# Attention pipeline of a two-layer gated cross-attention kernel: from four stages to five, on one Trainium2 core

## The reference

```python
x = x + jnp.tanh(g_xattn[0]) * _L0_xattn_ref(_layernorm(x, axis=-1), ctx_1024, ...)   # rotated q and k
x = x + jnp.tanh(g_ffn[0]) * _L0_ffn_ref(...)      # 8 experts, best 2 of 8
x = x + jnp.tanh(g_xattn[1]) * _L1_xattn_ref(...)  # normed context, gated result
x = x + jnp.tanh(g_ffn[1]) * _L1_ffn_ref(...)      # ternary weights
```

## Time and profile before

| | us |
|---|---|
| median of 3 runs | 3047.76 (3045.49 to 3053.43) |
| the profiled execution, own time | 3043.93 |
| its span, first to last instruction | 3042.1 |
| busy PE, DVE, ACT, POOL in the span | 2019.0, 1762.6, 1315.4, 1003.7 |
| mean granted clock of PE | 0.809 |
| layer 0 attention, first statistics to last result | 12.07 to 786.6 |
| layer 1 attention, likewise | 1552.1 to 2345.1 |

### The profile page before, as it was taken

One profiled execution on the slowest core, in us unless ns is written; L12 is line 12 of the kernel. 1 busy time (PEld: TensorE's weight loads), 2 busy tenths in 40 slices (PEclk: granted clock), 3 DMA queues, 4 the chain that ended last, 5 costly groups with the idle time before them and its releaser, 6 DMA issues. The chain is left out here.

```text
span 3042.1 us, 49795 instructions
## 1 busy us (share of the span) xinstructions
PE 2019.0 (66%) x14617; PEld 1560.7 (51%) x14617; DVE 1762.6 (58%) x3650; ACT 1315.4 (43%) x2345; POOL 1003.7 (33%) x1096
## 2 busy tenths in 40 slices
PE   5777677777543199999938788887886334444443
PEld 4555555555433199999825566665664222222222
DVE  5666666666454233333225555555553898988887
ACT  3444333344211044444324444444443566666665
POOL 0000100001266522222243333333330465565554
PEclk8988888888655599999968999999998566666666
DMA  2111111110443322222243333333331000000000
GB/s 68 40 36 43 36 39 36 37 43 26 141 154 125 123 76 87 87 87 87 77 82 65 69 80 71 69 68 67 76 70 56 17 27 28 28 21 28 28 25 17
DMA packets 177265, 185.56 MB, mean 61 GB/s; under 512 B 23745, under 2 KB 170946, under 8 KB 176130
## 3 DMA queue, kind: packets, MB, share of 16 engines
q1 hardware_dynamic: 152578, 149.49, 16.5%
q0 software_dynamic: 24576, 34.62, 5.6%
HBM read 109.82 MB, written 74.24 MB: 61 GB/s over the span
## 5 line engine op out<-in xcount | busy, mean ns | idle before, releaser
L527 DVE TENSOR_REDUCE a_mneg<-a_ps_s 128x8 f32<-128x960 f32 x256 | 285.8, 1151 | 63.0 <-PE a_ps_s L681 62.5
L681 PE MATMUL a_ps_s<-a_k,a_q 96*128 96x240 bf16 x1024 | 189.5, 334 | 153.9 <-DVE a_of L538 149.6
L377 ACT ACTIVATE a_probs<-a_ps_s 120x1024 f32<-120x1024 f32 x256 | 250.2, 1018 | 84.3 <-PE a_ps_s L695 84.3
L1295 DVE TENSOR_TENSOR e_h<-e_s,e_ps_ab 128x256 f32<-128x256 f32 (+1 forms) x213 | 89.4, 420 | 293.4 <-ACT e_s L1121 293.4
L1086 POOL TENSOR_TENSOR e_h_lo<-e_h 128x256 bf16<-128x256 f32 (+1 forms) x213 | 130.2, 611 | 326.0 <-DVE e_h L1295 326.0
L1314 PE MATMUL e_ps_ab<-e_xt_hi,e_w_hi 128*128 128x256 bf16 (+1 forms) x852 | 232.8, 273 | 0.1
L1314 PE MATMUL e_ps_ab<-e_xt_hi,e_w_lo 128*128 128x256 bf16 (+1 forms) x852 | 232.7, 273 | 0.0
L1314 PE MATMUL e_ps_ab<-e_xt_lo,e_w_hi 128*128 128x256 bf16 (+1 forms) x852 | 232.7, 273 | 0.0
L313 POOL TENSOR_TENSOR a_ve<-a_mv,a_eps 128x2 f32<-128x2 f32 x32 | 6.2, 195 | 664.7 <-DVE a_mv L506 664.7
L681 PEld LDWEIGHTS a_ps_s<-a_k,a_q 96*128 96x128 bf16 x1024 | 118.0, 121 | 195.2 <-DVE a_of L538 104.8
L341 POOL DMA_INDIRECT a_xa<-back_rows,a_where x128 | 202.2, 1580 | 45.8 <-issue 44.3
(11 more groups left out here) (237 smaller groups left out, 5430.8 us busy)
## 6 DMA issues: line engine op xcount, KB each, us to landing
e_xe<-sent_rows SPq DMA_DIRECT2D x71, 272.0 KB, 2.8
back_rows<-e_yo SPq DMA_DIRECT2D x71, 256.0 KB, 2.1
x_rows<-a_x SPq DMA_DIRECT2D x64, 256.0 KB, 3.2
a_xa<-in_x SPq DMA_DIRECT2D x32, 256.0 KB, 2.7
a_xr<-in_x SPq DMA_DIRECT2D x32, 256.0 KB, 2.9
e_xa<-x_rows SPq DMA_DIRECT2D x8, 1024.0 KB, 10.6
a_xa<-x_rows SPq DMA_DIRECT2D x32, 256.0 KB, 2.8
x_rows<-a_xa SPq DMA_DIRECT2D x32, 256.0 KB, 2.6
```

The costliest lines, as they stand in the source:

```text
L377: nc.scalar.activation(probs[0:S, 4 * g:4 * g + 4, :].rearrange("p h n -> p (h n)"), ps_s[0:S, g % 2, :, :].rearrange("p a n -> p (a n)"), ...
L527: nc.vector.tensor_reduce(mneg[:, g // 2, 8 * (g % 2):8 * (g % 2) + 8].rearrange("p (a h) -> p a h", a=2), ps_s[:, g % 2, :, 0:4 * S].rear ...
L681: last = nc.tensor.matmul(ps_s[:, g % 2, j // 2, (j % 2) * 2 * S:(j % 2 + 1) * 2 * S], q2[0:96, back.par, c, t * P:(t + 1) * P], k2[0:96, ...
```

## The change

The stages become *pre*, *front*, *mid*, *back*, *tail* (and *soon* in layer 1). The max scores, their maxima and the turning of the maxima are *mid*, a step ahead of *back*. The normed rows are transposed and copied at the end of *pre*, into `xt`, which now has two buffers; in layer 1 the gate projection is computed in *mid*. `ps_s` is split into `ps_m` for max scores and `ps_e` for scores and products, two banks each; the turned product goes to `ps_t` and `ps_x`. Max scores, maxima, scores and exponentials are done in eight groups of half the size rather than four. POOL takes over `xn` (and `cn`, the normed context of layer 1) and, in layer 0, the sums `qf` and `kf` of the rotation. The copy of the upper half of `q2` goes from DVE to ACT. A semaphore step `ready` is one small instruction on POOL. Every engine's order is written anew. Semaphore names change with the stages. The core of the diff follows; of the last piece, the order on PE, only the lines that stand in the new kernel are shown, not the removed ones. `turn_back` is the turning of `raw`, `turn_result` that of the divided result, `weigh` the product with the values, `gate_rows` the gate projection, `top` a maximum (DVE), `divided` the division, `gated` the gating.

```diff
-        ps_s = psum("ps_s", [P, 2, 2, 512])
+        ps_m = psum("ps_m", [P, 2, 512])
+        ps_e = psum("ps_e", [P, 2, 512])
...
-                pipeline(eng, lambda *batches: step(None, *batches), 4, 6)
+                pipeline(eng, lambda *batches: step(None, *batches), 5, 6)
             else:
-                pipeline(eng, step, 5, 6)
+                pipeline(eng, step, 6, 8)
...
+                ng.wait(gp, pre, "rstd")
+                ne.wait(gp, pre.back(1), "xT")
+                if not first:
+                    fe.wait(gp, pre.back(1), "cT")
+                nc.gpsimd.tensor_tensor(ready[:, :], half[:, 0:1], half[:, 0:1], ALU.mult).then_inc(ng.sem, 1)
+                for t in range(NT):
+                    last = nc.gpsimd.tensor_scalar(xn[:, t, :], xa[:, p, t, :], mv[:, t, 0:1], rstd[:, t:t + 1],
+                                                   ALU.subtract, ALU.mult)
+                if not first:
+                    last = nc.gpsimd.tensor_scalar(cn[0:S, :], ca[0:S, p, :], mv[0:S, NT, 0:1], rstd[0:S, NT:NT + 1],
+                                                   ALU.subtract, ALU.mult)
+                last.then_inc(ng.sem, 1)
+
+            def rotated(front):
+                fv.wait(gp, front, "q_sin1")
+                fa.wait(gp, front.back(1), "q_hi")
+                fv.wait(gp, front.back(1), "q_lo")
+                nc.gpsimd.tensor_tensor(qf[:, :, :], rc[:, :, :], rs[:, :, :], ALU.add).then_inc(fr.sem, 1)
+                fv.wait(gp, front, "k_sin1")
+                fa.wait(gp, front.back(1), "k_hi")
+                fv.wait(gp, front.back(1), "k_lo")
+                nc.gpsimd.tensor_tensor(kf[0:S, :], k_cos[0:S, :], k_sin[0:S, :], ALU.add).then_inc(fr.sem, 1)
...
-            def step(soon, pre, front, back, tail):
+            def step(soon, pre, front, mid, back, tail):
                 if tail is not None and first:
                     add_bias(tail)
                 if soon is not None and not first:
                     gp.wait_ge(x_ld[soon.par], 16 * (soon.half + 1))
                     gp.wait_ge(w_ld[soon.par], 16 * (soon.half + 1))
                     gather(soon, 0)
+                if front is not None and first:
+                    rotated(front)
+                if pre is not None:
+                    norms(pre)
+                if soon is not None and not first:
                     merged(gp, soon, 0)
                     gather(soon, 1)
-                if pre is not None:
-                    norms(pre)
...
+                def exp(i):
+                    be.wait(act, back, f"sc{i}")
+                    be.wait(act, back.back(1), "pv")
+                    nc.scalar.activation(probs[0:S, 2 * i:2 * i + 2, :].rearrange("p h n -> p (h n)"), ps_e[0:S, i % 2, :],
+                                         ACT.Exp, scale=SCALE).then_inc(ba.sem, 1)
...
+                if f and not first:
+                    context()
+                if b:
+                    exp(0)
+                    exp(1)
+                if f:
+                    queries()
+                if b:
+                    exp(2)
+                    exp(3)
+                if f:
+                    keys()
+                if b:
+                    exp(4)
+                    exp(5)
+                if t:
+                    result()
+                if b:
+                    exp(6)
+                    exp(7)
+                if f:
+                    values()
+                    columns()
+                if b:
+                    turned_raw()
+                if m and not first:
+                    gating()
+                if m:
+                    maxima()
+                if pre is not None:
+                    rows()
...
+                if b:
+                    spread_maxima()
+                if m:
+                    top(0)
+                    top(1)
                 if n:
-                    statistics(pre)
-                if n:
-                    normalise(pre)
+                    statistics()
+                if f and first:
+                    rotate_queries()
+                if m:
+                    top(2)
+                    top(3)
+                if f and first:
+                    rotate_keys()
+                if t:
+                    divided(0)
+                    divided(1)
+                    if not first:
+                        gated()
+                if f:
+                    split_queries()
+                    split_keys()
+                if m:
+                    top(4)
+                    top(5)
+                if m:
+                    top(6)
+                    top(7)
+                    halves()
+                if f:
+                    key_columns()
+                if t:
+                    finish()
...
+                def turn_back(i):
+                    if i == 0:
+                        ba.wait(pe, tail, "raw")
+                        da.wait(pe, back, "mT")
+                    else:
+                        if not first:
+                            da.wait(pe, back, "gate")
+                        if f:
+                            na.wait(pe, front, "x")
                         else:
-                            bv.wait(pe, back.back(1), "o")
+                            tv.wait(pe, tail.back(1), "sum")
+                    to = (ps_t, ps_x)[i]
+                    for g in range(H // GH):
+                        last = nc.tensor.transpose(to[:, g * P:(g + 1) * P], raw[:, g, i * P:(i + 1) * P], ident[:, :])
+                    last.then_inc(te.sem, 1)
...
+                def turn_rows():
+                    ng.wait(pe, pre, "norm")
+                    if m and not first:
+                        da.wait(pe, mid, "gate")
+                    elif t:
+                        tv.wait(pe, tail, "sum")
                     else:
-                        bv.wait(pe, back, f"top{g - 2}")
-                    for j in range(4):
-                        c = 4 * (g % 2) + j
-                        last = nc.tensor.matmul(ps_s[:, g % 2, j // 2, (j % 2) * 2 * S:(j % 2 + 1) * 2 * S],
-                                                q2[0:96, back.par, c, t * P:(t + 1) * P],
-                                                k2[0:96, back.par, 2 * c:2 * c + 2, :].rearrange("p j s -> p (j s)"),
+                        na.wait(pe, pre.back(1), "x")
+                    transposed(ps_x, xn).then_inc(ne.sem, 1)
...
+                def scores(i):
+                    if i == 0:
+                        bv.wait(pe, back, "m_all")
+                    if i < 2:
+                        ba.wait(pe, back.back(1), "raw")
+                    else:
+                        ba.wait(pe, back, f"exp{i - 2}")
...
+                if t:
+                    turn_back(0)
+                    turn_back(1)
                 if f:
+                    if not first:
+                        turn_context()
+                    project_rows()
                 if b:
                     scores(0)
                     scores(1)
+                if m:
+                    max_scores(0)
+                    max_scores(1)
                 if f:
+                    project_context()
+                for i in (2, 4):
+                    if b:
+                        scores(i)
+                        scores(i + 1)
+                    if m:
+                        max_scores(i)
+                        max_scores(i + 1)
+                if t:
+                    turn_result()
+                if b:
+                    scores(6)
+                    scores(7)
+                if m:
+                    max_scores(6)
+                    max_scores(7)
+                if f:
+                    turn_keys()
+                if t:
+                    project_result()
+                if b:
+                    weigh()
+                if f:
+                    turn_queries()
+                if m:
                     if not first:
+                        gate_rows()
+                    turn_maxima()
+                if pre is not None:
+                    turn_rows()
```

506 lines of the change are left out of this document (218 added, 288 removed).

## The result

The changed kernel takes 3145.64 us (median of 4 runs, 3144.35 to 3149.93), the kernel before 3049.76 (4 runs, 3045.49 to 3053.43): a ratio of 1.0317, with a 95% interval of 1.0299 to 1.0335.

The account below looks back on a forecast made before the run. It took a chain of waits, no full engine, to bound each step. Walks plus ports and clock gave -14 us in layer 0, +27 in layer 1; with fill and drain, +18 us, so 3065 us, range 2985 to 3135.

Parts of the forecast that it names:

- the walks: Stage-by-stage timings of one new step along PE, DVE, POOL and ACT: 21.7 us in layer 0, 23.4 in layer 1.
- The walk of layer 0: Layer 0's new step, timed from the first turning of `raw` to the next: 21.7 us against 23.54 before.
- the ports: DVE slowed by POOL's `xn` beside the splits or gate: 0.4 us a step in layer 0, 0.3 in layer 1.
- the clock: PE's dense work slowed by a lower clock after the sparse stretch: 1.0 us a step in both layers, bounds 0 and 3.0.
- The walk of layer 1: Layer 1's new step, ending with PE alone, then gate copy and maxima on ACT: 23.4 us against 23.82 before.
- `xn` on POOL: Normed rows computed on POOL: about 0.4 to 0.7 us each, costing nothing because hidden.
- The cover: Slack hiding `xn` in layer 0: it ends by some 13 us, PE turns rows at 19; without it, 1 to 2 us a step.
- Fill and drain: Cost of one more pipeline stage at the start and end of the layers: +2 and +3 us.
- POOL late: Rival: a 2x slower query sum on POOL delays queries, third exponential and PE's fifth group in layer 0; 3105 us, chance 0.07.
- The waits named ahead: PE's expected waits: some 3.7 us a step at layer 0's fifth score group, near 2 at layer 1's turning of `og`.
- The forecast's own test: A sign that the forecast is wrong: PE's waits add up to under 4 us in either layer.
- The clock that falls each step and stays low: Rival: low clock through PE's dense part, periods 25.1 and 26.7 us, 3190 us; chance 0.20 shared with POOL late.

Follow-up runs that it names:

- e1: The changed kernel with four buffers for the values instead of two, so their copy waits for a product two steps back; 3026.60 us.
- e2: Control: the changed kernel with its loop unrolled by four as in e1, but two value buffers and the old wait kept; 3143.21 us.
- e9: e5 with extra repeated matmuls in PE's waits in both layers; 2917.94 us, ratio 0.9572 to the kernel before.
- e5: e1 with `raw` copied ahead of the queries' columns on ACT and one half of those columns back on DVE; 2977.37 us.
- e6: e1 with ten extra matmuls a step in layer 1 alone, where PE waits for `og`; 2996.71 us.
- e4: The changed kernel with the normed rows and context back on DVE instead of POOL; 3136.63 us.
- e8: The kernel before with only the rotation's sums moved to POOL; 3009.35 us, ratio 0.9873 to the kernel before.
- e7: e1 with the rotation's two sums back on DVE; 3076.73 us.

## Why the prediction was wrong

**The step that failed** is the end of the walks: "PE runs on: keys 0.5, result 1.8, values 1.9, half the query transposes 0.5: 18.3. ACT copies both halves of `q2`" in layer 0, and "Then PE alone: 0.5 + 1.8 + 1.9 + 1.0 (queries) + 3.4 (gate) = 8.6" in layer 1. Both take it that ACT had copied the values and the key columns while PE was busy with keys and result. The wait for `pv` of `front.back(2)` stood in the diff, unchanged, and I read it with the stages of before. With it the copy starts when the product ends (2024.57 and 2024.50 us in the step shown). The term left out is the wait of the values and what stands behind it: put at nothing, measured at 1.41 and 2.34 us a step. e1 takes the wait away with nothing else, against e2: 1.41 us a step in layer 0, 2.34 in layer 1, 31 x 3.75 = 116 us of the 117 measured. Without that wait the kernel comes out at 3027: the forecast of 3065 would have been 38 us too high, inside the range but wrong in sign, since e1 is faster than the kernel before. The sign that was hit is luck.

**The other terms,** by e1, which has the step as I walked it:
- *The walk of layer 0*, 21.7, plus 0.4 for the ports and 1.0 for the clock, 23.1: e1 measured 21.98, 1.1 less. The clock was sized about right, if e1 has the 0.91 that e9 gained on e5, another kernel. Then walk and ports, 22.1 in the forecast, are 21.98 - 0.91 = 21.1: an estimate by which the walk was 0.6 too long and the ports 0.4.
- *The walk of layer 1*, 23.4: e6, whose projection runs at full clock, measured 23.45. The clock, 1.0: 24.41 - 23.45 = 0.96. With 0.3 for the ports the forecast was 24.7, e1 24.41.
- *The ports*, 0.4 and 0.3: e4, with `xn` on DVE again, puts it where DVE waited anyway, for the key columns; it gave 0.14 us a step in layer 0 and nothing in layer 1. DVE's own groups take the same time with `xn` on POOL as without: 219 and 221 ns for the copy of the keys, 684 and 685 for the second part of the queries (layer 0), 692 and 692 for `og` (layer 1). So no clash shows in the places where the prediction had it, and the term should have been near nothing. The Trainium skill (SBUF — State Buffer, "Who interferes with whom") describes an exclusive lock between VectorE and GpSimd. A clash can be seen in e8, where DVE's copy of the keys takes 1.01 us beside POOL's sum and 0.22 without it.
- *`xn` on POOL* was put at 0.4 to 0.7 us and takes 1.2. The cover of some 6 us held, so it cost nothing that e4 could show, as said.
- *Fill and drain* were put at 5 us. In the profiled executions 16 us lie outside the 31 periods of both layers, 12 of them ahead of the first copy of the maxima in layer 0.
- *POOL late*: the rival held that the queries' chain over the sum sets layer 0, 1.26 us a step if the sum took twice as long. e7 takes that very sum to DVE, where it needs 0.69 us in place of 1.26, and the step gets 1.5 us longer. The walk itself had DVE's list as what ends last (13.6), and the rival did not follow it.
- *The waits named ahead*, 3.7 us at the fifth score group and near 2 at `og` (1.7), were right to 0.3 us or better, and so was their cause. The sum `qf` on POOL was late by 1.26 us, as taken from the bias sum of the same size.
- *The forecast's own test*, PE waits under 4 us in either layer, did not strike: PE stood idle 5.9 us a step in layer 0 and 5.1 in layer 1. The clock of 0.86 and 0.88 is near the 0.85 named. None of the signs named could have caught the missing wait, except the periods themselves, 24.7 named and 26.86 measured in layer 1.

**The sums of the rotation** were right within the walk but never priced by themselves, and the expectations of e7 and e8 show that I would have priced them wrongly. By the four kernels without the wait, the rest of the change costs about 26 us (e7 against before, 18 to 36 by its interval), the sums on POOL bring 42 to 50 (e8 against before, e1 against e7), and the wait for the values costs 117 (e2 against e1).

**The rivals.** The clock that falls each step and stays low (3190) was nearer in time than the forecast, for another reason: the clock's term was about right, and the time came from a wait on ACT's list that nobody priced. That no rival said so is the second fault; I had listed waits on PE and DVE, and none on ACT's list.

## What to carry to other kernels

When a pipeline gets a stage more, every wait on a buffer of two (`back(2)`) must be read again with the new stages: which step holds that batch's last use now, and which engine's list stands behind it. A walk through a step should go down each engine's list and write the released time of every wait beside it, also of waits that the diff doesn't touch. PE's waits of 1.8 and 3.5 us a step ahead of dense work cost more than their length here, 0.9 to 1.0 us a step by the clock behind them, and harmless repeated matmuls in such a gap won this back. Work can be worth taking off a loaded engine even if the other does it at about half the pace: the two sums brought 42 to 50 us here.

## What the runs showed of the hardware

- A subtraction and a multiplication with two numbers per partition takes 1217 ns on POOL for 128x256 f32 and 410 on DVE, three times as long; the sum of two tensors of 120x256 takes 726 ns against 420, that of 128x512 1262 against 690, under twice. The Trainium skill (GPSIMD Engine Reference, "Engine selection") has about 2x for the second, which agrees. For an operation with one tensor as input the same row of that section says roughly line rate; the first, with 1217 ns against 410, does not agree.
- More work made the kernel faster: ten matmuls more a step, 30 us less (e6). In the steps shown the granted clock was 0.50 behind PE's wait of 1.76 us (2007.0 to 2013.5 us in e1) and 1.00 where 0.73 us of it were left (2015.8 to 2022.6 us in e6).
- The low clock of a periodic program can come in a pattern longer than one step. In the changed kernel's layer 0 the same projection takes 3.52 and 1.89 us in turn; in e2, the same work in a longer loop body, about three of four are slow. What chooses the pattern was not found.
- A copy of 120x256 bf16 on DVE took 1.01 us beside a sum of two tensors on POOL (e8) and 0.22 us without it.
